# Another order of the head transposes, and of the work around them, in the first layer of a two-layer attention kernel

## The reference

```python
x = x + L0(_gn(x))          # this layer's row loop is the one that changes
x = x + L1(_gn(x))          # banded attention, 4 heads

def L0(x1d):                 # one image: M=128 rows of N=256 tokens, 256 channels
    x = layernorm(x1d, norm_w, norm_b)
    qkv = (x @ qkv_w.T).reshape(M, N, 32, 3 * 8)      # 8 heads of 32
    q, k, v = (qkv[..., :8], qkv[..., 8:16], qkv[..., 16:])
    aff = einsum('bmich,bmjch->bmijh', q, k)          # within each row
    gate = sigmoid(x @ gate_w.T + gate_b)
    bias = x2d @ x2d_w.T / sqrt(32)
    w = softmax(aff + bias[:, None], axis=-2)
    out = einsum('bmrch,bmirh->bmich', v, w) * gate
    return out @ final_w.T + final_b
```

## Time and profile before

| | |
|---|---|
| median of 3 runs | 3649.43 us (3649.16 to 3661.97) |
| the profiled execution's own time | 3664.15 us |
| its span | 3662.3 us |
| TensorE's mean granted clock | 0.969 of full speed |

### The profile page before, as it was taken

The page is one execution under the profiler, slowest core; times in us unless marked ns, Lnnn a source line. Parts: engine busy times, 40 slices in busy tenths (PEclk is TensorE's granted clock), DMA queues, the critical chain, the costliest instruction groups (busy, mean ns, idle before and its releaser), DMA issues.

```text
span 3662.3 us, 122873 instructions
## 1 busy us (share of the span) xinstructions
PE 3372.3 (92%) x36747; PEld 3007.4 (82%) x36747; DVE 3002.9 (82%) x10850; ACT 2776.3 (76%) x8999; POOL 2177.9 (59%) x4107
## 2 busy tenths in 40 slices
PE   4459999999999999999999999799999999999999
PEld 1148888888888888888888888699999999999998
DVE  4458988888888888888888888688888888888887
ACT  1148888988888888888888988567667677776776
POOL 0047777777777777787777777444444444444443
PEclk7569999999999999999999999899999999999999
DMA  9921111111111111111111111011111111111111
GB/s 341 349 100 54 46 49 51 44 52 45 50 52 43 52 46 48 52 43 52 46 48 50 44 52 44 30 53 52 52 52 52 52 53 54 53 52 52 52 52 47
DMA packets 189032, 238.42 MB, mean 65 GB/s; under 512 B 11824, under 2 KB 176176, under 8 KB 184752
## 3 DMA queue, kind: packets, MB, share of 16 engines
q1 hardware_dynamic: 184368, 204.17, 17.7%
q10 hardware_dynamic: 4608, 33.56, 2.5%
HBM read 170.57 MB, written 67.11 MB: 65 GB/s over the span
## 4 chain that ended last, share of the span: by engine, by line
PE 58%; ACT 14%; issue 11%; DMA 6%; DVE 6%; POOL 2%; DVEq 1%; SPq 1%; ACTq 1%; POOLq 0%
PE work L477 24%; ACT prob L722 7%; PE work L486 7%; PE turn L527 5%; PE score L617 5%; PE mix L650 4%; DMA x_chunk<-xT 4%; PE mix L539 3%; PE score L505 3%; DMA x_tok<-x_nat 3%; PE turn L634 3%; ACT xnT L741 2%; ACT probT L728 2%; PE turn L635 2%; PE turn L636 2%
## 5 line engine op out<-in xcount | busy, mean ns | idle before, releaser
L364 POOL TENSOR_SCALAR prob<-prob,row_inv 128x256 f32<-128x256 f32 x2048 | 1068.0, 540 | 206.1 <-DVE row_inv L932 204.9
L722 ACT ACTIVATE prob<-prob,row_min 128x256 f32<-128x256 f32 x2048 | 1028.1, 507 | 128.3 <-DVE row_min L926 123.6
L477 PE MATMUL work<-src,w 128*128 128x256 f32 x7680 | 1067.5, 288 | 10.4 <-DVE src L915 6.7
L477 PEld LDWEIGHTS work<-src,w 128*128 128x128 f32 x7680 | 951.0, 189 | 12.3 <-DVE src L915 7.4
L415 POOL TENSOR_SCALAR prob<-prob,row_inv 128x160 f32<-128x160 f32 x1024 | 391.0, 401 | 767.4 <-DVE row_inv L1042 767.4
L926 DVE CUSTOM_DVE_ANT_0 prob<-score,neg_bias 128x256 f32<-128x256 f32 x2048 | 749.5, 417 | 17.2 <-PE score L505 10.1
L527 PE MATMUL turn<-ident,prob 128*128 128x128 f32 x3072 | 484.8, 280 | 120.0 <-ACT probT L728 101.4
L789 ACT ACTIVATE prob<-prob,row_min 128x160 f32<-128x160 f32 x1024 | 431.4, 426 | 141.7 <-DVE row_min L1035 141.6
L527 PEld LDWEIGHTS turn<-ident,prob 128*128 128x128 f32 x3072 | 336.3, 141 | 233.2 <-ACT probT L728 125.6
L477 PE MATMUL work<-att,wf 128*128 128x256 f32 x3072 | 432.1, 290 | 4.4 <-DVE att L981 3.0
L486 PE MATMUL work<-w,src 128*128 128x256 f32 x3072 | 425.8, 288 | 0.0
(11 more groups left out here) (110 smaller groups left out, 6225.7 us busy)
## 6 DMA issues: line engine op xcount, KB each, us to landing
pair_chunk<-pairT ACTq DMA_DIRECT2D x32, 1024.0 KB, 8.0
x_chunk<-xT SPq DMA_DIRECT2D x32, 1024.0 KB, 8.5
x_tok<-x_nat SPq DMA_DIRECT2D x128, 256.0 KB, 3.3
x_sb<-xT SPq DMA_DIRECT2D x128, 256.0 KB, 3.4
x1T<-y_sb SPq DMA_DIRECT2D x128, 256.0 KB, 2.2
x_sb<-x1T SPq DMA_DIRECT2D x128, 256.0 KB, 2.9
outT<-y_sb SPq DMA_DIRECT2D x128, 256.0 KB, 2.2
prob<-w_d SPq DMA_DIRECT2D x1, 1024.0 KB, 8.2
```

What stands on the lines that cost most here:

```text
L364: pool.tensor_scalar(prob[:, h, ib], prob[:, h, ib], row_inv[:, h, ib:ib + 1], 1.0, ALU.mult, ALU.mult).then_inc(norm_done[0], 1)
L477: ins = pe.matmul(out[:, cb], w[:, of_w, kb, cols + cb * P:cols + (cb + 1) * P], x[:, of_x, kb], start=n == 0, stop=n == len(terms) - 1)
L722: act.activation(prob[:, h, ib], prob[:, h, ib], ACT.Exp, bias=row_min[:, h, ib:ib + 1], scale=-1.0, accum_out=row_sum[:, h, ib:ib + 1]).t ...
```

## The change

Layer 1 stays as it is. In layer 0 no work is added to or taken from a row; its order changes on five engines, and the waits with it.

- **TensorE.** Turns 1 and 6 go to the score bank in place of 3 and 7. The new order: q, scores 4 to 7, mixes, turns 0 and 1, xn transposes, k, turn 2, v, turn 3, scores 0 to 3 of the next row, turn 4, gate, turns 5 and 6, y, turn 7.
- **ScalarE.** Before: q cast, exps 3, exps 4, copy 0, xnT, source cast, exps 5, k cast, copy 2, att cast, exps 6, v copy, exps 7, copy 4, exps 0 of the next row, gate, exps 1, copy 6, exps 2. After: q cast, exps 3, exps 4, copy 0, exps 5, xnT, k cast, copy 2, source cast, exps 6, exps 7, copy 4, att cast, v copy, gate, copy 6, exps 0, 1 and 2 of the next row.
- **VectorE.** After: y sum, q low, mins 4, inverse 1, mins 5 and 6, att_sum, copy 1, mins 7, inverse 2, k low, split, copy 3, mins 0 of the next row, inverse 3, mins 1, att low, layer norm statistics, copy 5, the rest of the layer norm, mins 2 and 3, inverse 0, copy 7. Of the two `bn_stats` of a pair of rows, the first now stands ahead of k low in the row whose y sum ends the pair, and the second ahead of the y sum of the following row. Before, both stood at the end of every second row, mins 7 ahead of att_sum and copy 1, copy 3 ahead of split, att low ahead of mins 0, mins 2 ahead of copy 5, and mins 3 and inverse 0 ahead of the layer norm statistics.
- **GpSimd.** xn moves from the head of a row, ahead of norms 1, to the end of the row before it, ahead of norms 0: these two change places.
- **SyncE.** The load of `x_tok` moves ahead of the wait for the y sum and of the other two transfers, and so is issued about one row earlier.

```diff
             def rows(n, of, to):                       # SyncE
+                    if n == 0 and ahead.exists:
+                        wait(sp, gn_scaled, ahead.times(1, -1))
+                        sp.dma_start(x_tok[:, ahead.base % 2], ...)
                     if last.exists:
                         wait(sp, y_done[n], m.times(1 if n == 0 else CB))
...
-                    if n == 0 and ahead.exists:
-                        wait(sp, gn_scaled, ahead.times(1, -1))
-                        sp.dma_start(x_tok[:, ahead.base % 2], ...)
...
                 def scores(r, hg):                     # TensorE
-                    wait(pe, turn_done[0][1], r.times(PAIRS0, 2 * hg - 2))
+                    if hg == 0:
+                        wait(pe, turn_done[0][1], r.times(PAIRS0, -3))
+                    else:
+                        wait(pe, turn_done[0][0], r.times(PAIRS0, 0))
...
                 def turns(h):
                     to = turn[:]
-                    if h % HPG == HPG - 1:
+                    if h in (1, 6):
                         to = score[:, 0].rearrange("p b t -> p (b t)")
...
+                    if h == 0:
+                        wait(pe, turn_done[0][1], m.times(PAIRS0, 0))
+                    elif h == 1:
+                        wait(pe, min_done[0], m.times(TB * H0, TB * (HPG + 1)))
+                    elif h == 2:
+                        wait(pe, turn_done[0][0], m.times(PAIRS0, 1))
+                    elif h == 3:
+                        wait(pe, turn_done[0][0], m.times(PAIRS0, 2))
+                    elif h == 4:
+                        wait(pe, turn_done[0][1], m.times(PAIRS0, 2))
+                    elif h == 5:
+                        wait(pe, turn_done[0][0], m.times(PAIRS0, 3))
+                    elif h == 6:
+                        wait(pe, turn_done[0][1], m.times(PAIRS0, 2))
+                        if nxt.exists:
                             wait(pe, min_done[0], nxt.times(TB * H0, TB))
                     else:
+                        wait(pe, turn_done[0][1], m.times(PAIRS0, 3))
...
+                def out_stats(ob, r, pair):            # VectorE
+                    wait(dve, y_done[0], r.times(1, 1))
+                    apart(dve, dve_passed)
+                    at = slice(pair, pair + 1) if isinstance(pair, int) else bass.ds(pair, 1)
+                    dve.bn_stats(gstat1[:, ob, at], y_sb[:, ob].rearrange("p r t -> p (r t)")).then_inc(y_stats, 1)
...
+            dve.wait_ge(y_done[0], ROWS)               # behind the loop
+            dve.bn_stats(gstat1[:, 1, ROWS // 2 - 1:ROWS // 2], ...).then_inc(y_stats, 1)
```

More of the change, by code:

```diff
@@ L316, in body @@
                     last, far, ahead = m + -1, m + 3, m + 4
+                    if n == 0 and ahead.exists:
+                        wait(sp, gn_scaled, ahead.times(1, -1))
+                        apart(sp, sp_passed)
+                        sp.dma_start(x_tok[:, ahead.base % 2], x_tok_v[:, bass.ds(ahead.times(TB), TB), :]
+                                     ).then_inc(x_tok_in[ahead.base % 2], 16)
                     if last.exists:
@@ L395, in body0 @@
                     norms(m, 3)
+                if ahead.exists:
+                    wait(pool, ln_var_done, ahead.times(2, 2))
+                    apart(pool, pool_passed)
+                    pool.tensor_tensor(ln_rstd[:], ln_var[:], minus_half[:], ALU.pow).then_inc(ln_rstd_done, 1)
+                    wait(pool, ln_rstd_done, ahead.times(2, 1))
+                    pool.tensor_tensor(ln_off[:], ln_neg[:], ln_rstd[:], ALU.mult).then_inc(ln_rstd_done, 1)
+                    wait(pool, ln_rstd_done, ahead.times(2, 2))
+                    wait(pool, t2_done, ahead.times(1, 0))
+                    apart(pool, pool_passed)
+                    for tb in range(TB):
+                        pool.tensor_scalar(xn[:, tb], g_tok[:, ahead.base % 2, tb], ln_rstd[:, tb:tb + 1],
+                                           ln_off[:, tb:tb + 1], ALU.mult, ALU.add).then_inc(xn_done, 1)
                 if nxt.exists:
@@ L554, in body0 @@
                     turns(0)
+                    turns(1)
                 if far.exists:
@@ L577, in body0 @@
                     project_tokens(work[:, 1], w0, 2 * CH, x).then_inc(v_ps[0], 1)
+                if m.exists:
+                    turns(3)
+                if nxt.exists:
                     scores(nxt, 0)
@@ L585, in body0 @@
                     turns(5)
+                    turns(6)
                 if last.exists:
@@ L735, in body0 @@
                     exps(m, 4)
-                    turn_copy(0)
+                    turn_copy(0, turn[:])
+                    exps(m, 5)
                 if far.exists:
@@ L743, in body0 @@
                                        ).then_inc(xnT_done, 1)
+                if nxt.exists:
+                    wait(act, k_ps[0], nxt.times(1, 1))
+                    act.copy(kT[:, nxt.base % 2, HIGH], work[:, 0]).then_inc(k_high[0], 1)
+                if m.exists:
+                    turn_copy(2, turn[:])
+                if far.exists:
                     wait(act, xnT_done, far.times(CB, CB))
@@ L747, in body0 @@
                 if m.exists:
[L748 to L753, removed]
+                    exps(m, 6)
+                    exps(m, 7)
+                    turn_copy(4, turn[:])
                 if last.exists:
@@ L967, in body0 @@
                 if m.exists:
-                    turn_copy(1, turn[:])
-                if m.exists:
+                    turn_copy(1, score[:, 0].rearrange("p b t -> p (b t)"))
+                    mins(m, 7)
                     inverse(m, 2)
+                if done.exists and done.base % 2 == 1:
+                    out_stats(0, done, done.times(1, 0, of=2))
                 if nxt.exists:
@@ L974, in body0 @@
                                       kT[:, nxt.base % 2, HIGH].bitcast(F32), ALU.subtract).then_inc(k_done[0], 1)
-                if m.exists:
-                    turn_copy(3, score[:, 0].rearrange("p b t -> p (b t)"))
                 if far.exists:
                     split_low(0, far, xnT[:])
[L979 to L982, removed]
+                if m.exists:
+                    turn_copy(3, turn[:])
                 if nxt.exists:
@@ L988, in body0 @@
                     mins(nxt, 1)
[L989 to L995, removed]
+                if last.exists:
+                    wait(dve, att_high[0], last.times(1, 1))
+                    dve.tensor_tensor(att[:, LOW], att_sum[:], att[:, HIGH].bitcast(F32), ALU.subtract
+                                      ).then_inc(att_done[0], 1)
                 if ahead.exists:
@@ L1002, in body0 @@
                 if m.exists:
-                    turn_copy(7, score[:, 0].rearrange("p b t -> p (b t)"))
+                    turn_copy(5, turn[:])
                 if ahead.exists:
@@ L1011, in body0 @@
                     dve.tensor_scalar(ln_var[:], ln_mv[:, :, 1], EPS, None, ALU.add).then_inc(ln_var_done, 1)
[L1012 to L1018, removed]
+                if nxt.exists:
+                    mins(nxt, 2)
+                    mins(nxt, 3)
+                    inverse(nxt, 0)
+                if m.exists:
+                    turn_copy(7, turn[:])
             over_rows(dve, 3, 2, body0)
+            dve.wait_ge(y_done[0], ROWS)
+            dve.bn_stats(gstat1[:, 1, ROWS // 2 - 1:ROWS // 2], y_sb[:, 1].rearrange("p r t -> p (r t)")).then_inc(y_stats, 1)
             dve.wait_ge(y_stats, CB * ROWS // 2)
```

48 lines of the change are left out of this document (8 added, 40 removed).

## The result

The changed kernel takes **3560.57 us** (median of 4 runs, 3558.29 to 3560.96), the kernel before 3653.14 in the runs beside it: a ratio of 0.9742, interval 0.9721 to 0.9763. The forecast was 3557.

A forecast was written before the change was run, and what follows sets the result against it. No engine is full, TensorE, VectorE and ScalarE nearly so; their order decides. Rows fall from 16.35 to 15.62 us (15.50 from alternating 15.28 and 15.72, plus contention), times 127 saves 93: 3557 us, range 3541 to 3586.

The forecast's parts named there:

- TensorE's floor: What TensorE would need for a layer 0 row without waits: 15.0 us, against 16.35 before the change.
- v held up by exps 5: On ScalarE exps 5 move ahead of xnT, on which v waits: v late by 0.28 us, floor 15.28 a row.
- The loop through VectorE: Scores of heads 0 to 3 to the same point next row: 14.94 us, 15.72 in every second row.
- Contention: VectorE instructions with two SBUF inputs and GpSimd's norms delay each other: average row 15.51 to 15.77 us, 15.62 taken.
- Copy 3: Split beside GpSimd can make copy 3 on VectorE late for turn 4: cost 0.03 to 0.27 us a row.
- Turn 1: In the score bank turn 1 waits for no copy: removes 0.54 us seen in one row of TensorE's timeline, more elsewhere.
- x_tok: Earlier load removes GpSimd's 179 us of waits, worth nothing by itself beyond the 10 us TensorE stood for GpSimd.
- xn: xn ahead of norms 0 on GpSimd: costs nothing; 0.6 us if the layer norm were 1 us later.
- the floor: Rival: exps 5 do not delay xnT and VectorE has slack; rows 15.0 to 15.3, 3478 to 3516 us, chance 0.11.
- no change: Rival: waits only move, ScalarE's idle 1.9 us a row stays; rows 16.2 to 16.5, 3631 to 3668 us, chance 0.11.
- copy 3's wait: Rival: turn 4 waits for copy 3 behind source cast and split; rows 15.9 to 16.2, 3592 to 3630 us, chance 0.17.
- the slower case: Rival: GpSimd becomes the bound, norms blocked in all four groups; rows 16.65 us, 3687 us, chance 0.09.

## Why the prediction was right, and where its steps were not

**The sum.** 15.62 a row forecast, 15.63 measured; 93 us saved by the forecast, 92.6 measured. (The middle of its bounds 15.51 and 15.77 is 15.64, not 15.62, which makes 2.5 us.) TensorE's floor of 15.0 stands: no version here got below it. The best that computes the same, with exps 5 behind xnT, needs (2201.2 - 235.5) / 127 = 15.48 (its first and last cast of q), att low from PSUM 15.42.

**v held up by exps 5: right.** 0.28 forecast, 0.27 a row measured by the standing of its weight loads, and moving exps 5 removes it.

**The loop through VectorE: right in kind.** Undoing the statistics' split cost 30 us, where 0.64 every second row would be up to 41. The forecast's alternation of two lengths was not seen, though: turn 7 ended after 15.38, 15.60, 15.78 and 15.61 us in four rows in a row. With att low from PSUM it is there: 15.26, 15.54, 15.25 and 15.55. So the short row is as forecast (15.28 without contention) and the long one is shorter than its 15.72; in the change a wait of every fourth row lies over both.

**Contention: right in kind, too small in the sum.** GpSimd's timeline shows norms 3 blocked once, and VectorE's shows att low waiting first:

```profile
1009.38 2.28 POOL L364 TENSOR_SCALAR prob<-prob,row_inv 128x256 f32<-128x256 f32 x4 [0.99 <-DVE row_inv L942]
```

```profile
1009.90 0.95 DVE L1006 TENSOR_TENSOR att<-att_sum,att 128x512 fp32r<-128x512 f32 x1
```

Att low took 0.95 instead of 0.68, so it first waited for a norm under way, and then blocked the next one (2.28 instead of 1.85). Head 6 is in the first two of those four norms. By the Trainium skill (SBUF — State Buffer, "Who interferes with whom") whichever instruction issues first holds the port pair to its end; the trace agrees here.

Turn 6 escapes only as long as att low comes late enough. TensorE stood for norms at turn 6 in 30 of some 122 rows, one in four, and one of those is this (GpSimd's norms 3, the second of them by itself, att low, and turn 6):

```profile
1040.32 2.35 POOL L364 TENSOR_SCALAR prob<-prob,row_inv 128x256 f32<-128x256 f32 x4 [1.01 <-DVE row_inv L942]
```

```profile
1040.78 0.98 POOL L364 TENSOR_SCALAR prob<-prob,row_inv 128x256 f32<-128x256 f32 x1
```

```profile
1040.78 0.72 DVE L1006 TENSOR_TENSOR att<-att_sum,att 128x512 fp32r<-128x512 f32 x1
```

```profile
1041.89 0.65 PE L538 MATMUL score<-ident,prob 128*128 128x128 f32 x4 [0.43 <-POOL prob L364]
```

Here att low begins 0.46 behind norms 3, where in the row above it was 0.52. It gets ahead of the second norm, which is head 6's, and turn 6 ends 1.08 behind turn 5 (1042.54 against 1041.46) where it needs 0.44. In all 30 such rows of the trace att low begins 0.45 or 0.46 behind norms 3 and the second norm is the long one; in the other rows it begins at 0.52 or later. With att low from PSUM this wait is gone, which shows the cause. What puts att low 0.06 earlier in every fourth row stays open; the loop's body holds four rows.

The forecast bounded turn 6's loss at 0.31 from norms 3 that start 1.08 behind the scores; in both rows read above they start 1.3 behind (1009.38 against 1008.06, 1040.32 against 1039.01), and where head 6 was blocked turn 6 lost 0.64. All contention was put at 0.12 a row (15.62 less 15.50); att low's alone measures 0.21 (15.63 less 15.42).

**Copy 3: small in the change.** Turn 4 lost 0.14 in the row shown, inside 0.03 to 0.27, and 0.01 in the row before it. As the next wait in line it came up as soon as v's was removed.

**Turn 1: right that its wait goes, wrong as a term by itself.** The text credited "the 0.54 seen in rows 3, and more" to the bank. Alone the bank brought nothing; on the kernel before, the next wait (the scores for copy 3) was ready to take its place. What the loops count is the sum over a whole row with all orders in place, and there the total was right. The steps that were listed as separate savings are not additive: alone they gave 0.5%, nothing and nothing, together 0.5%, with turn 3 moved 1.3% slower, and with all the orders 2.6% faster.

**x_tok: the step that failed.** "Worth nothing by itself beyond TensorE's 10 us there" was read from who waits in the kernel before. It brought 0.5% there (13 to 25 us), and in the changed order it is needed: without it the change would have been a loss. In both orders the loop from the transfer back to the y sum runs through turn 6. In the old one exps 0 and 1 and inverse 0 of the next row stood ahead of copy 6, so the loop went on by turn 7 and copy 7, and from turn 6 to the y sum were 2.65 us (the kernel before, in a row without `bn_stats`):

```profile
1008.52 0.60 PE L527 MATMUL turn<-ident,prob 128*128 128x128 f32 x4
```

```profile
1011.17 0.68 DVE L948 TENSOR_TENSOR y_sb<-work,x_sb 128x512 f32<-128x512 f32 x1
```

The new order puts them behind copy 6 and ahead of copy 7: with x_tok late, turn 6 to the y sum takes 4.07 (1012.41 to 1016.48). I checked the transfer against the old order only.

**xn: costed at nothing.** The move costs nothing, as forecast; undoing it costs 17 us, because the xn transposes then wait.

**Where the agreement is luck.** The loops of the sum are those of the new order, so what x_tok and xn are worth is not missing from it. But contention was put 0.09 too low or more, and the rows without att low's contention, 15.42, are shorter than the 15.50 that the sum had without any: the loop through VectorE was put too long. These two offset each other, so the agreement within 4 us is partly luck. Why that loop is shorter than its sum stays open.

**Of the rivals,** the floor and "no change" did not come about, copy 3's wait appeared at a fraction of its price, and the slower case is out: a norm took 522 ns on average, where blocking in all groups would be 700 (2.79 us for four).

Open: which of the remaining orders (ScalarE's, turns 6 and 7, the rest of VectorE's, xn) carries the last 2.2% was not separated. The waits that go between the two kernels are those for copy 2 and for att low.

## What to carry to other kernels

A wait that the profile names is a saving only up to the next wait behind it in the row; follow the whole loop from row to row, in the new order, before crediting a part. When the order of instructions changes, re-check what was off the critical path against the *new* order, transfers first: here a load that cost 0.5% in the old order would have cost 3.5% in the new one. Parts that are worthless or harmful alone can be what makes the others pay, so try parts both alone on the old kernel and undone on the new one.

## What the runs showed that was not expected

One VectorE instruction with two SBUF inputs can be held up by far more than one norm: split took 1.75 us with turn 3 behind v, where 0.68 is its usual least, while GpSimd ran the second half of g (1.29 us, two SBUF inputs):

```profile
1002.38 1.29 POOL L392 TENSOR_TENSOR g_tok<-g_tok,gn_row 128x512 f32<-128x512 f32 x1
```

Split began at 1002.46 and ended 0.54 behind the end of g. In the changed kernel that half of g takes 1.72 us when split runs beside it, and 1.28 when not. GpSimd's timeline of the changed kernel, in two rows, shows both:

```profile
1006.67 1.72 POOL L380 TENSOR_TENSOR g_tok<-g_tok,gn_row 128x512 f32<-128x512 f32 x1
...
1023.33 1.28 POOL L380 TENSOR_TENSOR g_tok<-g_tok,gn_row 128x512 f32<-128x512 f32 x1
```

The forecast's bound of 0.23 for VectorE was taken from one split beside norms (0.46 each). Beside norms it is nearly right, where att low lost 0.27 (0.95 against 0.68); beside g it does not hold.
